# Unread products between TensorE's last mixing product, two global maxima and the down projection, and a sixth quantised tile ahead of the first gate/up evacuation

## The chip, the cores and the metric

One core of one Trainium2 chip runs the whole kernel. The metric is device microseconds of one execution, from the first to the last instruction and what lies around them. The kernel before took 748.6 us (median of three runs, 746.82 to 748.89 us).

## The reference

The kernel computes one layer of a graph network on 1250 nodes of width 1024, in float32. The parts ahead of the change (layer norm, a graph convolution over 40000 edges, linear attention with 16 heads) end in the matrix `x2`, the sum of both branches and the input. The change lies behind that, in the quantised feed-forward part:

```python
    def _L0_ffn_ref(x, clip_x, clip_down, w_gate, w_up, w_down):
        def _act_fake_quant(x, clip_factor):
            scale = jax.nn.sigmoid(clip_factor) * jnp.max(jnp.abs(x)) / QMAX
            return jnp.clip(_ste_round(x / scale), -QMAX - 1.0, QMAX) * scale
        ...
        xq = _act_fake_quant(x, clip_x[0])
        gate = jnp.einsum('bsh,ih->bsi', xq, _weight_fake_quant(w_gate))
        up = jnp.einsum('bsh,ih->bsi', xq, _weight_fake_quant(w_up))
        h = _act_fake_quant(jax.nn.silu(gate) * up, clip_down[0])
        return jnp.einsum('bsi,hi->bsh', h, _weight_fake_quant(w_down))
```

The width inside is 352. Both activations are quantised with one scale for the whole matrix: the maximum over all 1250 rows has to be known before the first element can be rounded. These are the two global maxima.

## The kernel before

The nodes lie in ten tiles of 128 rows (`T`; the last has 98). Every engine has its own program (`@block.sync`, `gpsimd`, `tensor`, `scalar`, `vector`), runs it in order, and waits on semaphores. The order of the work is written out by hand.

**Mixing.** `tile_b` (L690 on TensorE, L1280 on VectorE) runs for each tile 40 aggregation products (L698) and 48 attention products (L724). VectorE moves the second result out at L1317, and forms the tile's row extremes (L1328). GpSimd computes one column at L482, VectorE ends with the largest deviation.

**First maximum.** After the last tile VectorE writes the per-row maxima onto a diagonal (L1336, semaphore `m_ready`). TensorE multiplies it with a matrix of ones (L738), which puts all 1250 row maxima in every partition of bank 2. VectorE reduces them (`broadcast_max`, L1350: L1353, L1354) and computes each tile's scale and shift (L1358, `xn_columns`).

**Quantising.** `xq_tile(t)` on VectorE (L1361) scales a tile to int8 (L1366) and casts it to bf16 (L1371, `q_ready`). For the tiles in `ON_ACT` (1, 5, 7, 9) ScalarE does the scaling (`affine`, L932, L936). Tiles 0 and 1 are transposed by TensorE (`xq_tile`, L741, L745) and moved by ScalarE (L941). Tiles 2 to 9 are transposed by DMA, issued by SyncE as soon as `q_ready` allows (L391).

**Gate and up.** There are twelve units, numbered by `UNIT` (L254): four groups of columns `NCH` (256 columns are tiles 0 and 1; 512 are tiles 2 to 5; 256 are 6 and 7; 226 are 8 and 9) by three blocks of the inner width. `gate_up(u)` on TensorE (L748) runs 8 products for gate and 8 for up (L763). The first unit of a group waits for all of the group's tiles, and unit u waits until unit u-2 has been moved out. ScalarE applies silu to the gate (L953), VectorE multiplies it with up (`up`, L1383, L1391) and takes the maximum (L1380). Two lists set the order of quantising and units: `PE_FFN` for TensorE and ScalarE, `DVE_FFN` for VectorE (L261, L262).

**Second maximum and down.** VectorE reduces the maxima of the units (L1399, L1400, `m_ready`), TensorE broadcasts them (L773), VectorE reduces (L1353) and quantises the first 128 columns (L1402, L1406, `hq_first`). ScalarE quantises the others (L964, L966). TensorE then runs six products for each tile (L785) into `y_bank`, eight banks in turn: 0, 1, 6, 7, 2, 3, 4, 5. VectorE moves each half out (L1415), and VectorE (L1418) and GpSimd (L491) add 304 and 720 of the 1024 columns to `x2`, which SyncE stores.

Bank 3 holds half of the down weights' scales until ScalarE has moved them out at L929 (semaphore `d_row`, awaited by TensorE at L729, in the last tile's mixing). After that nothing is in it until the third tile of the down projection.

Of the kernel before, what the change touches and what calls it, by code (L numbers as in the profile page):

```python
# [17 lines left out]
HALF = 512  # L18
N, D = 1250, 1024
T = -(-N // P)  # L20
# [33 lines left out]
def gps_layer(nc, x, src, dst, gnn_W, gnn_b, Wq, bq, Wk, bk, Wv, bv, Wo, bo,  # L54
              clip_x, clip_down, w_gate, w_up, w_down, out):
    with ExitStack() as ctx:
        def sb(name, shape, dt):
            return ctx.enter_context(nc.sbuf_tensor(name, shape, dt))

        def sems(*names):  # L60
            return {n: ctx.enter_context(nc.semaphore(n)) for n in names}

        bank = [ctx.enter_context(nc.psum_tensor(f"bank{i}", [P, HALF], F32)) for i in range(8)]
# [8 lines left out]
        def part(at, *dims, dt=F32):  # L72
            size = 1
            for d in dims:
                size *= d
            words = size * {F16: 2, BF16: 2, I8: 1}.get(dt, 4) // 4
            a = mem[:, at:at + words]
            if dt != F32:
                a = a.bitcast(dt)
            if len(dims) == 2:  # L80
                a = a.rearrange("p (a b) -> p a b", b=dims[1])
            if len(dims) == 3:
                a = a.rearrange("p (a b c) -> p a b c", b=dims[1], c=dims[2])
            return a
# [38 lines left out]
        wdT = part(at, FB, D, dt=BF16)  # L123
# [41 lines left out]
        ident16 = sb("ident16", [P, P], BF16)  # L165
# [4 lines left out]
        def col(n=1):  # L170
# [16 lines left out]
        S = sems("consts", "pool_step", "edges_in", "bias_in", "x_in0", "x_in1", "dve_step",  # L187
                 *[f"w_in{i}_{c}" for i in range(8) for c in range(2)], "ln_step", "var_ready", "rstd_ready", "edges_ready",
                 "edges_T", "columns", "scratch_set", "ln_done", "xT_full", "xT_hi", "xT_lo", "w_hi", "w_lo", "kv_full", "kv_evac",
                 "k_relu", "kv_done", "q_full", "x_hi", "x_lo", "xT_in0", "xT_in1", "src_gap", "hot_src_act", "counts_diag", "q_relu", "q_hi", "q_lo", "g_full", "h_hi", "h_lo", "hot_dst_ready",  # L190
                 "hot_src_ready", "adj_mm", "adj_added", "counts_set")
# [5 lines left out]
        SF = sems("raw_in0", "raw_in1", "wq_ready", "w16_ready", "wT_in0", "wT_in1", "diag", "drow_full")  # L197
# [3 lines left out]
        def over_tiles(tile):  # L201

            for t in range(T):
                tile(t, t % 2, t // 2)
# [45 lines left out]
        landed = [16 * sum(1 if kind == "gu" else 2 for kind, _, _ in pieces[i % 2:i + 1:2]) for i in range(len(pieces))]  # L250
# [3 lines left out]
        UNIT = [(c, b) for c in range(len(NCH)) for b in range(FB)]  # L254
# [4 lines left out]
        Q = [("q", t) for t in range(T)]  # L259
        U = [("u", u) for u in range(len(UNIT))]  # L260
        PE_FFN = Q[:2] + U  # L261
        DVE_FFN = Q[:5] + U[:1] + Q[5:6] + U[1:3] + Q[6:8] + U[3:4] + Q[8:] + U[4:]  # L262

        AFFINE_AFTER = {("q", 1): 5, ("u", 1): 7, ("u", 2): 9}
        ON_ACT = (1, 5, 7, 9)
# [230 lines left out]
        def _(pe):  # L496
# [131 lines left out]
            with pe.If(span >= W):  # L628
                with pe.Fori(1, WINDOWS) as k:
                    with pe.Fori(0, C) as c:  # L630
                        pe.wait_ge(SE["e_hot"], 2 * ((k - 1) * C + c) + 2)
                        pe.matmul(agg[0][:, 0:WC], hot_src[0:EC, 0, 0, :], hot_dst[0:EC, 0, 0, :], start=True,
                                  stop=True).then_inc(SE["e_mm"], 1)
# [28 lines left out]
            for n in range(2):  # L662
                for p in range(PAIRS):
                    i = PAIRS * n + p
# [7 lines left out]
                    for a, b in ((0, 0), (0, 1), (1, 0)):  # L672
                        last = pe.matmul(m_bank[i % 4][:, :], kvs[:, a * PAIRS + p, :], wo16[n][p // 4][:, 2 * (p % 4) + b, :],  # L673
                                         start=(a == b), stop=(a == 1))
# [15 lines left out]
            def tile_b(t, par, t2):  # L690
# [25 lines left out]
                for n in range(2):  # L716
# [11 lines left out]
                    if (t, n) == (T - 1, 0):  # L728
# [5 lines left out]
            most = pe.value_load(flags[0:1, 1:2], min_val=0, max_val=E + 1)  # L734
            over_tiles(tile_b)

            pe.wait_ge(SC["m_ready"], 1)
            pe.matmul(bank[2][:, P:P + LAST], ones_m[0:LAST, :], max_diag[0:LAST, 1, 0:LAST], start=True,  # L738
                      stop=True).then_inc(SC["m_all"], 1)

            def xq_tile(t):  # L741
                o = tp[t % 2][:, :].bitcast(BF16)
                pe.wait_ge(SC["q_ready"], t + 1)
                for k in range(K):
                    last = pe.transpose(o[:, k * P:(k + 1) * P], q16[t % 4][:, k * P:(k + 1) * P], ident16[:, :])  # L745
                last.then_inc(SC["qT_full"], 1)

            def gate_up(u):  # L748
                c, b = UNIT[u]
                (c0, w), n = NCH[c], FR[b]  # L750
                pair = (bank[0:2], bank[6:8])[u % 2]
                if b == 0:
                    for t in range(c0 // P, -(-(c0 + w) // P)):
                        if t < 2:
                            pe.wait_ge(SC["qT_moved"], t + 1)
                        else:
                            pe.wait_ge(SC[f"qT_in{t % 4}"], 16 * ((t + 2) // 4))
                if u >= 2:
                    pe.wait_ge(SC["silu"], u - 1)
                    pe.wait_ge(SC["up_moved"], u - 1)  # L760
                for m in range(2):
                    for k in range(K):
                        last = pe.matmul(pair[m][0:n, 0:w], wguT[:, 2 * k + m, b * P:b * P + n],  # L763
                                         xqT[:, k, c0:c0 + w], start=(k == 0), stop=(k == K - 1))
                    last.then_inc(SC["gate_full"], 1)

            pe.wait_ge(S["counts_diag"], T + 1)
            for i in (8, 9):
                pe.wait_ge(SF[f"wT_in{i % 2}"], landed[i])
            for what, i in PE_FFN:  # L770
                xq_tile(i) if what == "q" else gate_up(i)
            pe.wait_ge(SC["m_ready"], 2)
            pe.matmul(bank[2][:, 0:P], ones_m, max_diag[:, 0, :], start=True, stop=True).then_inc(SC["m_all"], 1)  # L773

            for t in range(T):
                if t == 0:
# [194 lines left out]
        def _(dve):  # L971
# [389 lines left out]
            def xq_tile(t):  # L1361

                if t in ON_ACT:
                    dve.wait_ge(SC["affine"], ON_ACT.index(t) + 1)
                else:
                    step(dve.tensor_scalar(q8[t % 4], x2[:, t, :], xn_scale[:, t:t + 1], xn_shift[:, t:t + 1], ALU.mult, ALU.add))  # L1366
                if t in (4, 5):
                    dve.wait_ge(SC["qT_full"], t - 3)
                elif t >= 6:
                    dve.wait_ge(SC[f"qT_in{t % 4}"], 16 * ((t - 2) // 4))  # L1370
                dve.tensor_copy(q16[t % 4], q8[t % 4]).then_inc(SC["q_ready"], 1)  # L1371
# [11 lines left out]
            def up(u):  # L1383

                c, b = UNIT[u]
                (c0, w), n = NCH[c], FR[b]
                if u == 0:
                    dve.wait_ge(SC["gus"], 1)
                dve.wait_ge(SC["gate_full"], 2 * u + 2)
                dve.wait_ge(SC["silu"], u + 1)  # L1390
                dve.scalar_tensor_tensor(hT[0:n, b, c0:c0 + w], (bank[1], bank[7])[u % 2][0:n, 0:w],  # L1391
                                         gus[0:n, FB + b:FB + b + 1], sg[0:n, u % 2, 0:w], ALU.mult,
                                         ALU.mult).then_inc(SC["up_moved"], 1)
                h_max(u)

            for what, i in DVE_FFN[1:]:
                xq_tile(i) if what == "q" else up(i)
# [43 lines left out]
```

## Time and profile before

| | us |
|---|---|
| median of three runs | 748.6 |
| lowest and highest | 746.82, 748.89 |
| the profiled execution's own time | 748.37 |
| its span, first to last instruction | 746.6 |
| last mixing product ends | 675.98 |
| first product of gate and up starts | 687.26 |
| last product of gate and up ends | 716.32 |
| first product of down starts | 720.08 |

The lower part of the table is in microseconds from the span's start, as all times in the timelines are. The granted clock is the share of full speed (2.4 GHz) that TensorE was given: 1.00 and 0.50 (1.2 GHz) are its two levels here, and the mean over the span is 0.982. "Idle before" says how long an engine had nothing to run, and the arrow names whose work ended that.

### The profile page before, as it was taken

The numbers are of one execution on the slowest core, as the hardware profiler recorded it, in microseconds if no ns is written. First come the engines' busy times: TensorE is split into PE (matmuls) and PEld (weight loads), VectorE is DVE, ScalarE is ACT, GpSimd is POOL, SyncE is SP. The second block draws the span as 40 slices with busy tenths as digits, with TensorE's granted clock in tenths as the row PEclk, the third lists the DMA queues.
The fourth block names the chain that finished last, engine by engine and source line by source line (L and its number), as shares of the span: only waits on it lengthen the run. The fifth ranks groups of instructions, "written<-read, shape, count | busy, mean of one in ns | idle before, by whom it ended". The sixth has DMA issues, their size and how long they took to land.

```text
span 746.6 us, 12015 instructions
## 1 busy us (share of the span) xinstructions
PE 708.0 (95%) x3772; PEld 361.7 (48%) x3772; DVE 495.0 (66%) x975; ACT 209.5 (28%) x346; POOL 272.0 (36%) x403
## 2 busy tenths in 40 slices
PE   4999999999999999999999999999999999995984
PEld 2455555555555554666644444444444444443651
DVE  7878887887666655656842213657777788756667
ACT  5133334643333244446212212500000000012350
POOL 5566677898666655540010000011111111110018
PEclk9999999999999999999999999999999999996988
DMA  9652422541000000003030300242222222001406
GB/s 343 216 134 65 100 48 65 172 168 57 0 0 0 0 2 1 2 0 113 1 113 0 113 0 0 88 118 71 68 64 62 60 59 70 28 6 31 82 26 249
DMA packets 52764, 52.18 MB, mean 70 GB/s; under 512 B 36482, under 2 KB 37514, under 8 KB 52720
## 3 DMA queue, kind: packets, MB, share of 16 engines
q1 hardware_dynamic: 52720, 51.61, 22.9%
q8 instruction: 26, 0.43, 0.2%
q14 instruction: 18, 0.15, 0.1%
HBM read 37.96 MB, written 5.12 MB: 58 GB/s over the span
## 4 chain that ended last, share of the span: by engine, by line
PE 68%; issue 13%; DVE 9%; POOL 4%; ACT 2%; DMA 2%; DVEq 1%; POOLq 0%; SPq 0%; ACTq 0%
PE bank L532 31%; PE bank L724 12%; PE bank L698 10%; PE bank L606 10%; POOL mem L491 2%; DVE mem L1014 2%; PE bank L517 2%; ACT mem L812 2%; PE bank L549 2%; DVE counts L1104 1%; DVE mem L1184 1%; DMA mem<-in_x 1%; PE bank L673 1%; DVE mem L1030 1%; DMA mem<-in_L_gnn_W 1%
## 5 line engine op out<-in xcount | busy, mean ns | idle before, releaser
L532 PE MATMUL bank<-mem 128*128 128x512 f16 x1440 | 327.6, 381 | 4.9 <-DVE mem L1030 1.7
L532 PEld LDWEIGHTS bank<-mem 128*128 (+1 forms) x1440 | 137.9, 98 | 158.5 <-issue 6.9
L443 POOL TENSOR_SCALAR hot_src<-iota_p,src_col 125x128 bf16<-125x128 bf16 x252 | 174.3, 706 | 14.1 <-issue 14.1
L1104 DVE TENSOR_TENSOR counts<-bank,counts 128x120 f32 x328 | 92.4, 282 | 49.1 <-issue 8.4
L606 PE MATMUL bank<-mem 128*128 128x512 f16 (+2 forms) x576 | 105.3, 339 | 0.8 <-DVE mem L1143 0.8
L724 PE MATMUL bank<-mem 128*128 128x512 f16 x480 | 105.4, 379 | 0.0
L698 PE MATMUL bank<-mem 128*128 128x512 f16 x400 | 88.0, 379 | 0.0
L606 PEld LDWEIGHTS bank<-mem 128*128 128x128 f16 (+1 forms) x576 | 55.2, 98 | 42.5 <-DVE mem L1143 1.4
L724 PEld LDWEIGHTS bank<-mem 128*128 128x128 f16 x480 | 47.0, 98 | 55.7
L832 ACT ACTIVATE src_gap<-iota_p,loT 125x128 bf16<-125x128 bf16 x84 | 33.7, 402 | 114.4 <-PE bank L517 105.8
L480 POOL TENSOR_TENSOR mem<-mem 128x1024 f32<-128x1024 f32 x10 | 23.5, 2348 | 114.4 <-DMA mem<-in_L_mix_bo 114.4
L482 POOL TENSOR_TENSOR cols<-cols 128x1 f32<-128x1 f32 x10 | 5.6, 555 | 159.7 <-DVE cols L1326 159.7
L698 PEld LDWEIGHTS bank<-mem 128*128 128x128 f16 x400 | 39.2, 98 | 47.0
L1235 DVE SCALAR_TENSOR_TENSOR mem<-bank,cols,mem 128x512 f16<-128x512 f32 x20 | 14.9, 750 | 67.6 <-ACT mem L896 67.6
L1091 DVE TENSOR_TENSOR hot_dst<-iota_w,keyT 125x480 bf16<-125x480 bf16 x84 | 55.1, 657 | 0.0
L440 POOL COPY src_col<-loT 125x3 f32 (+1 forms) x84 | 25.7, 305 | 69.7 <-PE bank L517 64.9
L1014 DVE SCALAR_TENSOR_TENSOR mem<-mem 128x2048 f16<-128x2048 f32 x16 | 36.8, 2304 | 6.8 <-ACT mem L812 6.8
L896 ACT ACTIVATE mem<-bank,cols 128x512 f16<-128x512 f32 x20 | 13.8, 689 | 86.1 <-PE bank L532 76.6
L1317 DVE SCALAR_TENSOR_TENSOR mem<-bank,mem 128x512 f32<-128x512 f32 x20 | 13.8, 692 | 36.3 <-PE bank L724 36.0
L491 POOL TENSOR_TENSOR mem<-mem 128x720 f32<-128x720 f32 (+1 forms) x10 | 18.7, 1897 | 45.7 <-DVE mem L1415 45.7
L812 ACT ACTIVATE mem<-mem 128x2048 f16<-128x2048 f32 x16 | 30.4, 1906 | 15.4 <-DMA mem<-in_L_mix_Wk 6.1
L835 ACT ACTIVATE hot_src<-src_gap,cols 125x128 bf16<-125x128 bf16 x84 | 33.9, 404 | 2.7
(148 smaller groups left out, 644.4 us busy)
## 6 DMA issues: line engine op xcount, KB each, us to landing
mem<-in_x SPq DMA_DIRECT2D x18, 512.0 KB, 3.8
out_x<-mem SPq DMA_DIRECT2D x9, 512.0 KB
mem<-in_L_mix_Wk SPq DMA_DIRECT2D x4, 1024.0 KB, 9.5
mem<-in_L_mix_Wv SPq DMA_DIRECT2D x4, 1024.0 KB, 8.6
mem<-in_L_mix_Wq SPq DMA_DIRECT2D x4, 1024.0 KB, 5.2
mem<-in_L_gnn_W SPq DMA_DIRECT2D x4, 1024.0 KB, 5.2
mem<-in_L_mix_Wo SPq DMA_DIRECT2D x2, 2048.0 KB, 7.9
mem<-in_L_ffn_w_down SPq DMA_DIRECT2D x4, 352.0 KB, 3.1
```

The costliest lines, as they stand in the source:

```text
L443: pool.tensor_scalar(hot_src[0:EC, i, c, :], iota_p[0:EC, :], src_col[0:EC, i, c:c + 1], None, ALU.is_equal).then_inc(S["hot_src_ready"], 1)
L491: pool.tensor_tensor(x2[:, t, s], x2[:, t, s], y_t[t % 4][:, s], ALU.add).then_inc(SC["y_ready1"], 1)
L532: last = pe.matmul(o[:, :], xT[:, a * K + k, bass.ds(t * P, P)], w16[i][:, k, b, :], start=(at == 0), stop=(at == len(parts) - 1))
L606: last = pe.matmul(proj[j % 2][:, 0:w], w_q.rearrange("p a n -> p (a n)"), xT[:, a * K + k, t0 * P:t0 * P + w], start=(k == 0 and a == b), ...
L698: last = pe.matmul(agg[n][:, :], a_t[par][:, s, :], h16[:, s, b * D + n * HALF:b * D + (n + 1) * HALF], start=(fresh and s == 0 and b == 0 ...
L724: last = pe.matmul(proj[n][:, :], q_k, m16[b][:, k, n * HALF:(n + 1) * HALF], start=(k == 0 and a == b), stop=(k == K - 1 and a == 1))
L812: act.activation(w16[i][:, 4 * c:4 * c + 4, 0, :], w_raw[i][:, 4 * c:4 * c + 4, :], ACT.Copy, scale=W_UP).then_inc(S["w_hi"], 1)
L832: act.activation(src_gap[0:EC, i, :], iota_p[0:EC, :], ACT.Abs, bias=loT[0:EC, bass.ds(g * G + G - 1, 1)], scale=-1.0).then_inc(S["src_gap ...
L835: act.activation(hot_src[0:EC, i, G - 1, :], src_gap[0:EC, i, :], ACT.Relu, bias=ones[0:EC], scale=-1.0).then_inc(S["hot_src_act"], 1)
L1014: dve.scalar_tensor_tensor(w16[i][:, s, 1, :], w_raw[i][:, s, :], W_UP, w16[i][:, s, 0, :], ALU.mult, ALU.subtract).then_inc(S["w_lo"], 1)
L1091: dve.tensor_tensor(hot_dst[0:EC, i], iota_w[0:EC], key, ALU.is_equal).then_inc(S["hot_dst_ready"], 1)
L1104: dve.tensor_tensor(window, agg[i][:, k * WC:(k + 1) * WC], window, ALU.add).then_inc(S["adj_added"], 1)
```

## The change

It defines `keep_busy(n)`: n products of 128 x 512 (`ident16` as weights, the first 512 columns of the down weights `wdT` as the moving operand) that are written to bank 3 and that nobody reads. TensorE runs 19 of them between the last mixing product and L738, 11 between L738 and the transposes of tiles 0 and 1, 5 between these and the first unit, 6 before L773 and 6 after it. TensorE's waits for the constants and the last weight transposes (L767 to L769) come ahead of the first 19, since these read both. In `DVE_FFN` the sixth quantised tile comes ahead of unit 0 rather than behind it.

```diff
-        DVE_FFN = Q[:5] + U[:1] + Q[5:6] + U[1:3] + Q[6:8] + U[3:4] + Q[8:] + U[4:]
+        DVE_FFN = Q[:6] + U[:3] + Q[6:8] + U[3:4] + Q[8:] + U[4:]
...
+            def keep_busy(n):
+
+                for _ in range(n):
+                    pe.matmul(bank[3][:, :], ident16[:, :], wdT[:, 0, 0:HALF], start=True, stop=True)
+
+            pe.wait_ge(S["counts_diag"], T + 1)
+            for i in (8, 9):
+                pe.wait_ge(SF[f"wT_in{i % 2}"], landed[i])
+            keep_busy(19)
             pe.wait_ge(SC["m_ready"], 1)
...
-            pe.wait_ge(S["counts_diag"], T + 1)
-            for i in (8, 9):
-                pe.wait_ge(SF[f"wT_in{i % 2}"], landed[i])
-            for what, i in PE_FFN:
-                xq_tile(i) if what == "q" else gate_up(i)
+            keep_busy(11)
+            for i in range(2):
+                xq_tile(i)
+            keep_busy(5)
+            for u in range(len(UNIT)):
+                gate_up(u)
+            keep_busy(6)
             pe.wait_ge(SC["m_ready"], 2)
             pe.matmul(bank[2][:, 0:P], ones_m, max_diag[:, 0, :], start=True, stop=True).then_inc(SC["m_all"], 1)
+            keep_busy(6)
```

The order of TensorE's instructions from the last mixing product to the down projection; the kernel before, where L724 is mixing, L738 and L773 are the two maxima, L745 the transposes, L763 gate and up, L785 down:

```order
L724 MATMUL bank<-mem 128x512 x24
L738 MATMUL bank<-mem 128x98
L745 MATMUL bank<-ident,mem 128x128 x16
L763 MATMUL bank<-mem 128x256 x32
...
L763 MATMUL bank<-mem 96x226 x16
L773 MATMUL bank<-mem 128x128
L785 MATMUL bank<-mem 128x512 x60
```

The same place in the changed kernel (its line numbers are 9 to 12 higher; L740 are the unread products):

```order
L724 MATMUL bank<-mem 128x512 x24
L740 MATMUL bank<-mem,ident 128x512 x19
L747 MATMUL bank<-mem 128x98
L740 MATMUL bank<-mem,ident 128x512 x11
L754 MATMUL bank<-ident,mem 128x128 x16
L740 MATMUL bank<-mem,ident 128x512 x5
L772 MATMUL bank<-mem 128x256 x32
...
L772 MATMUL bank<-mem 96x226 x16
L740 MATMUL bank<-mem,ident 128x512 x6
L784 MATMUL bank<-mem 128x128
L740 MATMUL bank<-mem,ident 128x512 x6
L797 MATMUL bank<-mem 128x512 x60
```

Five groups, 47 products in all, stand between the others; nothing else on TensorE moved.

VectorE in the kernel before, from the cast of tile 3 on (L1366 and L1371 quantise, L1391 and L1380 evacuate a unit):

```order
L1371 CAST mem<-mem 128x1024
L1366 TENSOR_SCALAR mem<-mem,cols 128x1024
L1371 CAST mem<-mem 128x1024
L1391 SCALAR_TENSOR_TENSOR mem<-bank,cols,mem 128x256
L1380 TENSOR_REDUCE cols<-mem 128x1
L1371 CAST mem<-mem 128x1024
L1391 SCALAR_TENSOR_TENSOR mem<-bank,cols,mem 128x256
```

The same in the changed kernel (the lines are 12 higher):

```order
L1383 CAST mem<-mem 128x1024
L1378 TENSOR_SCALAR mem<-mem,cols 128x1024
L1383 CAST mem<-mem 128x1024 x2
L1403 SCALAR_TENSOR_TENSOR mem<-bank,cols,mem 128x256
L1392 TENSOR_REDUCE cols<-mem 128x1
L1403 SCALAR_TENSOR_TENSOR mem<-bank,cols,mem 128x256
```

The cast of tile 5 stands directly behind that of tile 4 instead of behind unit 0. SyncE's order is the same in both kernels.

## Rows read from the trace of the kernel before

**Rows 1.** The page: busy time of each engine.
```profile
PE 708.0 (95%) x3772; PEld 361.7 (48%) x3772; DVE 495.0 (66%) x975; ACT 209.5 (28%) x346; POOL 272.0 (36%) x403
```
**Rows 2.** Stretches of 0.5 us: length, engines' busy time, PEclk, DMA share, GB/s.
```profile
678.00:678.50 0.50, 0.00 (x0) 0.00 (x0) 0.50 (x2) 0.00 (x0) 0.41 (x1) 0.76 0.00 0
...
691.50:692.00 0.50, 0.50 (x4) 0.37 (x3) 0.50 (x2) 0.00 (x0) 0.00 (x0) 0.58 0.24 48
...
719.00:719.50 0.50, 0.00 (x0) 0.00 (x0) 0.50 (x3) 0.01 (x1) 0.00 (x0) 0.72 0.00 0
...
726.00:726.50 0.50, 0.50 (x4) 0.23 (x3) 0.50 (x3) 0.50 (x1) 0.25 (x1) 0.95 0.00 0
```
**Rows 3.** Timeline around the first maximum: start, length, engine, line, operation, idle before.
```profile
673.66 2.32 PE L724 MATMUL bank<-mem 128*128 128x512 f16 x10
...
680.50 0.75 PE L738 MATMUL bank<-mem 98*128 98x98 f32 x2 [4.52 <-DVE mem L1336]
681.36 0.39 DVE L1353 TENSOR_REDUCE cols<-bank 128x1 f32<-128x226 f32 x1 [0.84 <-PE bank L738]
...
683.28 0.69 DVE L1371 CAST mem<-mem 128x1024 bf16<-128x1024 int8 x1
...
684.12 1.87 PE L745 MATMUL bank<-ident,mem 128*128 128x128 bf16 x16 [2.87 <-DVE mem L1371]
```
**Rows 4.** Timeline from the transposes to the first unit of 512 columns.
```profile
685.17 1.94 ACT L941 ACTIVATE mem<-bank 128x1024 bf16<-128x1024 bf16 x2 [1.55 <-PE bank L745]
...
687.00 1.24 ACT L936 ACTIVATE mem<-mem,cols 128x1024 int8<-128x1024 f32 x1
...
687.26 7.66 PE L763 MATMUL bank<-mem 128*128 128x256 bf16 x48 [1.27 <-ACT mem L941]
...
688.43 0.69 DVE L1371 CAST mem<-mem 128x1024 bf16<-128x1024 int8 x1
...
690.93 0.48 DVE L1391 SCALAR_TENSOR_TENSOR mem<-bank,cols,mem 128x256 f32<-128x256 f32 x1 [1.81 <-PE bank L763]
...
691.79 0.68 DVE L1371 CAST mem<-mem 128x1024 bf16<-128x1024 int8 x1
...
695.91 4.26 PE L763 MATMUL bank<-mem 128*128 128x512 bf16 x19 [1.00 <-DMA mem<-mem]
```
**Rows 5.** The DMA transposes of the quantised tiles (L391), one line's view.
```profile
L391 SPq DMA_TRANSPOSE mem<-mem x8: 1231/1232/1521, 686.3 to 703.8; - x8
...
DMA to landing us min/median/max: 3.1/3.2/3.3
```
**Rows 6.** Timeline: 48 products of 512 columns in a row at full clock.
```profile
645.80 10.52 PE L724 MATMUL bank<-mem 128*128 128x512 f16 x48
```
**Rows 7.** Timeline from the last units to the second maximum and the down projection.
```profile
699.80 16.52 PE L763 MATMUL bank<-mem 128*128 128x512 bf16 x126
...
717.80 0.49 PE L773 MATMUL bank<-mem 128*128 128x128 f32 x2 [1.48 <-DVE mem L1400]
718.32 0.29 DVE L1353 TENSOR_REDUCE cols<-bank 128x1 f32<-128x128 f32 x1 [0.58 <-PE bank L773]
...
720.08 16.12 PE L785 MATMUL bank<-mem 128*128 128x512 bf16 x60 [1.79 <-DVE mem L1406]
...
721.52 0.84 ACT L966 ACTIVATE mem<-mem 128x768 bf16<-128x768 int8 x1
721.58 0.75 DVE L1415 SCALAR_TENSOR_TENSOR mem<-bank,cols,mem 128x512 f32<-128x512 f32 x1 [1.56 <-PE bank L785]
...
723.69 1.87 POOL L491 TENSOR_TENSOR mem<-mem 128x720 f32<-128x720 f32 x1 [45.04 <-DVE mem L1415]
...
726.25 16.79 POOL L491 TENSOR_TENSOR mem<-mem 128x720 f32<-128x720 f32 x9 [0.69 <-DVE mem L1415]
726.47 1.40 DVE L1415 SCALAR_TENSOR_TENSOR mem<-bank,cols,mem 128x512 f32<-128x512 f32 x2
```

## The prediction

> **What bounds the kernel now.** The page comes first: TensorE is busy for 708.0 of 746.6 us [rows 1], so nearly everywhere it sets the pace, and only its gaps and its clock are open to a change like this. Next the granted clock in stretches of 0.5 us [rows 2]. In the part that the change touches it falls twice. The first fall is in the stretch 678.0 to 678.5 us, with TensorE idle since 675.98 [rows 3]; the clock is back only at 691.9. The second fall is between 719.0 and 719.5, after an idle time that only L773 interrupted for 0.49 us [rows 7]; it is back at 726.0. In both cases TensorE then runs real work at 1.2 GHz: L738, the transposes and the first units of gate and up, and later two tiles of the down projection. Last the timelines, to see which of this ends a wait.
>
> Around the first maximum everything is one chain: product L738, VectorE's reduction and scaling, the first cast, the transposes, ScalarE's move, and gate/up at 687.26 [rows 3, 4]. TensorE then runs three units of 256 columns, and waits 1.00 us for a DMA before the first unit of 512 columns at 695.91 [rows 4]. That DMA is the transpose of tile 5. Behind it TensorE has no gap until 716.32 [rows 4, 7]. So all that matters of the first half is how far the start at 695.91 moves. In the down projection GpSimd's addition starts at 723.69, idles once for 0.69 us until 726.25, and then runs nine tiles without a gap [rows 7]; VectorE keeps the same pace of 1.9 us for a tile. There the end is set by when the first two tiles are delivered.
>
> **The unread products themselves.** At full clock a product of 512 columns takes 10.52 / 48 = 0.22 us [rows 6]. Nineteen are 4.2 us: from 675.98 to 680.2, and L738 could not start before 680.50 anyway. This is hidden, with 0.3 us to spare. L738 then ends near 680.9; eleven are 2.4 us, to 683.3, and the first cast delivers tile 0 not before 683.6 (below). Five are 1.1 us behind the second transposes (685.0 to 686.1), while ScalarE is still moving. Six are 1.3 us in the 1.48 us gap before L773, and six again in the 1.79 us gap behind it [rows 7]. All 47 lie in gaps and cost nothing as long as the clock is full. Without that cover each costs its own 0.22 us, or 0.43 us at half clock, because TensorE runs in order. Their bank is free until the third tile of down, and the weights whose landing is now awaited earlier were transposed long before. I take the bank, the operands and the moved waits at nothing.
>
> **The first chain at full clock.** If the unread products keep the clock up:
> - L738 to the reduction took 0.86 us at half clock (680.50 to 681.36) [rows 3]. The same step at full clock is L773, 0.52 us (717.80 to 718.32) [rows 7]. Gain 0.34, which moves VectorE's whole quantising earlier by as much: the casts of tiles 0 to 4 stand back to back with their scalings. The cast of tile 0 ends at 683.97 - 0.34 = 683.63.
> - Eight transposes are 8 x 0.107 us at half clock and half that at full: 0.43 less ahead of ScalarE's first move. From the cast's end to ScalarE was 1.20 us (683.97 to 685.17) [rows 3, 4], and becomes 0.78, so ScalarE starts at 684.4. Its two moves take 1.94 us together, as before, and gate/up starts at 684.4 + 1.94 + 0.15 = 686.5 rather than 687.26.
> - A unit of 256 columns is 16 products: 3.5 us at half clock, 1.75 at full. Unit 0 ends at 688.25, unit 1 at 690.0. Unit 2 needs unit 0 moved out.
>
> **The moved tile.** VectorE's cast of tile 4 ended at 689.12 [rows 4], now 688.8. The next instruction is the cast of tile 5, 0.68 us, whose scaling ScalarE ends at 688.24 at the latest [rows 4], so it ends at 689.5. It used to stand behind unit 0 and ended at 692.47. Unit 0 is moved out from 689.5 to 690.0 instead of from 690.93: the cast ahead of it delays it, by up to 0.7 us against an evacuation in the old order at full clock. It holds back unit 2, which starts at 690.1 instead of 690.0, and units 1 and 2 end at 690.0 and 691.8. What is queued behind it on VectorE (units 1 and 2, tiles 6 and 7) is needed by TensorE only for unit 6, more than 10 us later. So the step costs nothing by itself.
>
> SyncE issues the transposes one behind the other, 1.23 us each, and each lands 3.2 us after its issue [rows 5]. Tile 4 is issued at 688.8, so tile 5 can follow at 690.05 and not at 689.5; it lands at 693.25. With 0.15 us for the wait, unit 3 starts at **693.4**, where it started at 695.91: gain **2.5 us**. Between bounds: if the transfers get in each other's way (they used to be 1.45 us apart, and 5 follows 4 after 1.25) it can be 0.5 us less; if SyncE's issue doesn't hold tile 5 back, 0.5 us more; and the very most is 4.1 us, when TensorE itself is ready at 691.8. I take 2.5, since both durations in it are rows of the same instruction.
>
> Behind unit 3 everything is TensorE's own time. Tiles 6 and 7 move out earlier with the rest, and the second maximum comes 2.5 us earlier.
>
> **The down projection at full clock.** VectorE started on the first half at 721.58, 1.50 us after the first product: three products at half clock (1.28) and 0.22 until seen. Now it is 3 x 0.22 + 0.2 = 0.86, i.e. 720.94 in the old times. The second half is complete 0.66 us later, VectorE has moved both by 722.35, and GpSimd starts at 722.42 instead of 723.69: 1.27 earlier. The second tile comes 1.9 us later, at 724.3, instead of at 726.25: **1.9 us** earlier, and the 0.69 us of idle time are gone. VectorE, whose third tile started at 726.47, starts it at 720.94 + 2 x 1.9 = 724.74, **1.7 us** earlier. The pace of 1.9 us for a tile remains, and becomes the bound from the first tile on. ScalarE's quantised columns for tiles 2 and 3 are ready at 722.36 [rows 7], and TensorE wants them at 720.08 + 12 x 0.22 = 722.72, so the next thing that is late has 0.36 us to spare. I take 1.8.
>
> **Sum.** 2.5 + 1.8 = 4.3 us. The profiled execution took 748.37 us, so 744.1; its own time lies 0.2 below the median of the runs (748.6), and I predict **744.2 us**, 0.6% less. A measurement of this kernel can tell about 0.3% (2.2 us) from no change; the three runs before lie 2.1 us apart.
>
> **Rivals.**
> 1. *The clock is lost in one of the two places.* The products leave gaps of 0.3 to 0.6 us, and around the transposes TensorE runs only about 0.45 us at a time: from 683.3 to 686.5 it is busy for about 2.0 of 3.2 us. L773 alone did not keep the clock at its fall of 719 [rows 2, 7]. For holding: after the third unit of 256 columns TensorE idled 1.00 us and the clock stayed [rows 2, 4]. If it is lost around the transposes, units 0 to 2 run largely at half clock as before, unit 3 waits for TensorE (686.9 + 7.8 = 694.7) and gains about 1.1; with down, 2.9, so 745.5. If it is lost around the second maximum, only the 2.5 remain: 745.9. The Trainium skill ("TensorE: Matmul & The Clock Gate", "A second HAM failure mode: psum-queue depth-cycling") describes a kernel whose short idles between groups of products made the clock swing between its levels; by that rule the outcome here would be this rival's 745.5 to 745.9. The trace does not bear it out: with 0.2 to 1 us idle at a time it shows no fall.
> 2. *Neither gap is held and only the order pays.* The products end before the awaited signals, and the clock falls in what is left. Then tile 5 is early but TensorE is not ready before 695.1 (687.26 + 7.66, and the wait): 0.8 to 1 us, so 747.5. Against it: the gaps left are a tenth of those at which it fell.
> 3. *Slower: the unread products run at half clock and stand in the way.* Were the clock to fall at 678.25 as before, ten products would be done and nine would take 0.43 each: L738 starts at 682.1, 1.6 late. Eleven take 4.7 us and five 2.15, so gate/up starts near 691.6; even at full clock from there unit 3 starts at 696.9, 1.0 late. Around the second maximum six take 2.6 us in 1.5 and in 1.8: 1.1 and 0.8 late. Together 2.9 slower, 751.3. It decides from the point where 19 products outlast 4.5 us, 0.24 us each. Against it: products of this very shape in the mixing keep the clock at 1.00, at 0.22 each, and these follow without a gap.
> 4. *More than forecast:* the transpose of tile 5 lands as soon as TensorE is ready, 691.9: 4.0 + 1.8, 742.5. Against it the issue time.
>
> **How the numbers follow.** Forecast 0.68; rival 1 0.14, rival 2 0.08, rival 3 0.05, rival 4 0.05. The forecast's own range is 743.2 to 745.2 (0.5 us for the landing, 0.2 for down, the rest the scatter of a median). To hold 8 in 10 the range takes in most of rivals 1 and 4: 742.6 to 746.4. Faster by more than 0.3% is below 746.4: the forecast, rival 4 and two thirds of rival 1, 0.82. Within 0.3%: rival 2 and the rest of rival 1, 0.13. Slower: 0.05.
>
> **What would show it.** The granted clock stays at 1.00 from 676 us to the end of the down products. Fifteen or more of the first nineteen products take 0.22 us each, and L738's successor starts within 0.1 us of the signal. Gate/up starts 0.7 to 0.8 us earlier, unit 0's evacuation stands behind the cast of tile 5, and unit 3 starts at 693.4, still released by a DMA. GpSimd has no idle time between its first two additions. I am wrong if a stretch between 683 and 687, or the one before down, shows 0.50; if unit 3 is released by TensorE's own work; or if the last additions end less than 3.5 us earlier.

## The result, and the profile after

The changed kernel took 745.92 us (median of 15 runs, 744.61 to 747.70), the kernel before 748.40 us in the 15 runs beside them. The ratio is 0.9971, with a 95% interval of 0.9964 to 0.9979: 0.29% less, at the very edge of what the prediction called distinguishable. 744.2 us was predicted, in a range of 742.6 to 746.4. The time lies in the range, but not in the forecast's own 743.2 to 745.2; the gain is 2.5 us, and 4.2 to 4.3 were forecast. So the question is where 1.8 us went.

The page says that TensorE was busier, and clocked higher: the mean granted clock over the span is 0.992 instead of 0.982.

```profile
PE 713.9 (96%) x3819; PEld 363.7 (49%) x3819; DVE 494.7 (66%) x975; ACT 208.8 (28%) x346; POOL 270.9 (36%) x403
```

The timeline of the changed kernel around the first maximum (start, length, engine, line, operation, idle before). L740 are the unread products, L747 answers to L738, L754 to L745, L953 to L941 and L772 to L763 of [rows 3, 4]:

```profile
671.66 4.05 PE L724 MATMUL bank<-mem 128*128 128x512 f16 x18
...
675.54 4.26 PE L740 MATMUL bank<-mem,ident 128*128 128x512 bf16 x19
...
680.23 0.47 PE L747 MATMUL bank<-mem 98*128 98x98 f32 x2 [0.43 <-DVE mem L1348]
...
680.53 2.54 PE L740 MATMUL bank<-mem,ident 128*128 128x512 bf16 x11
680.80 0.39 DVE L1365 TENSOR_REDUCE cols<-bank 128x1 f32<-128x226 f32 x1 [0.56 <-PE bank L747]
...
683.48 0.62 PE L754 MATMUL bank<-ident,mem 128*128 128x128 bf16 x8 [0.41 <-DVE mem L1383]
...
684.13 1.94 ACT L953 ACTIVATE mem<-bank 128x1024 bf16<-128x1024 bf16 x2 [1.07 <-PE bank L754]
...
684.73 1.24 PE L740 MATMUL bank<-mem,ident 128*128 128x512 bf16 x5
...
686.21 5.41 PE L772 MATMUL bank<-mem 128*128 128x256 bf16 x48 [0.24 <-ACT mem L953]
```

The last mixing product ends at 675.71 here and at 675.98 before [rows 3], so 0.27 us are to be taken off every comparison of starts. With that, everything up to gate/up is as forecast: the unread products end in time, L747 hands over after 0.57 us instead of 0.86, ScalarE starts 0.77 us earlier (684.13 for 685.17), and gate/up starts 0.78 us earlier. Three units take 5.41 us instead of 7.66.

What follows is not. The same timeline on, from the evacuation of unit 0 to the start of unit 3, answering to [rows 4]:

```profile
687.87 1.29 DVE L1383 CAST mem<-mem 128x1024 bf16<-128x1024 int8 x2
...
689.08 0.48 DVE L1403 SCALAR_TENSOR_TENSOR mem<-bank,cols,mem 128x256 f32<-128x256 f32 x1
...
694.39 9.83 PE L772 MATMUL bank<-mem 128*128 128x512 bf16 x37 [2.77 <-DMA mem<-mem]
```

TensorE is through with unit 2 at 691.62 and then waits 2.77 us for the transpose of tile 5; before, it waited 1.00. The view of the transposes' line, of which the first four are those that unit 3 needs, says that one of them took 4.8 us, and SyncE's issue of one 2.3 us; [rows 5] had 3.3 and 1.5 as the largest:

```profile
L391 SPq DMA_TRANSPOSE mem<-mem x8: 1232/1320/2297, 685.7 to 704.0; - x8
...
DMA to landing us min/median/max: 3.2/3.2/4.8
```

The granted clock (columns as in [rows 2]) is 1.00 from 676 to 695.5 us, through both gaps that the change fills. Then it falls, in a place where it had not fallen before:

```profile
695.50:696.00 0.50, 0.50 (x3) 0.17 (x2) 0.00 (x0) 0.00 (x0) 0.00 (x0) 0.72 1.11 213
...
699.00:699.50 0.50, 0.50 (x3) 0.24 (x2) 0.00 (x0) 0.00 (x0) 0.00 (x0) 0.86 0.00 0
```

TensorE had idled 2.77 us and had then worked for 1.3. From 695.7 to 699.1 unit 3 runs at 1.2 GHz, eight products at twice 0.22 us.

Around the second maximum and in down the clock is 1.00 and the timeline is as forecast. The answer to [rows 7]:

```profile
718.29 1.46 PE L740 MATMUL bank<-mem,ident 128*128 128x512 bf16 x6
...
720.25 13.21 PE L797 MATMUL bank<-mem 128*128 128x512 bf16 x60 [0.50 <-DVE mem L1418]
...
721.11 1.41 DVE L1427 SCALAR_TENSOR_TENSOR mem<-bank,cols,mem 128x512 f32<-128x512 f32 x2 [0.92 <-PE bank L797]
...
722.59 18.70 POOL L491 TENSOR_TENSOR mem<-mem 128x720 f32<-128x720 f32 x10 [44.23 <-DVE mem L1427]
```

GpSimd's ten additions now have no gap. From the first product of down to the end of the last addition it was 22.96 us (720.08 to 743.04) and is 21.04: 1.92 less.

The account of the two profiled executions (spans 746.6 and 744.8 us): 0.27 ahead of the change, 1.25 earlier at unit 3 (695.91 against 694.39, less the 0.27), 1.68 lost again up to the end of the units (20.41 us from unit 3 to 716.32 before, 22.09 to 716.48 now), 1.92 gained in down. Together 1.76, and the spans differ by 1.8. In this pair of executions the first half of the change was thus worth minus 0.4 us, and all of the gain is the second half's. The changed kernel's profiled execution took 746.61 us, 0.7 more than its median, so others lost less.

### The profile page after: what moved, and what is told of

Its sections match the earlier page's. It is cut to its first block, busy times and chain, and to the rows that moved or that the text cites. A ratio compares the mean times of both kernels' runs of the same rounds, so it can differ in the third digit from the quotient of the medians.

```text
span 744.8 us, 12108 instructions
## 1 busy us (share of the span) xinstructions
PE 713.9 (96%) x3819; PEld 363.7 (49%) x3819; DVE 494.7 (66%) x975; ACT 208.8 (28%) x346; POOL 270.9 (36%) x403
## 4 chain that ended last, share of the span: by engine, by line
PE 69%; issue 12%; DVE 9%; POOL 4%; ACT 2%; DMA 2%; DVEq 1%; POOLq 0%; SPq 0%; ACTq 0%
PE bank L532 31%; PE bank L724 13%; PE bank L698 10%; PE bank L606 10%; POOL mem L491 2%; DVE mem L1026 2%; PE bank L517 2%; ACT mem L824 2%; PE bank L549 2%; DVE counts L1116 1%; DVE mem L1196 1%; PE bank L673 1%; DMA mem<-in_x 1%; DVE mem L1042 1%; DMA mem<-in_L_gnn_W 1%
## 5 line engine op out<-in xcount | busy, mean ns | idle before, releaser
L724 PE MATMUL bank<-mem 128*128 128x512 f16 x480 | 105.4, 379 | 0.0
L724 PEld LDWEIGHTS bank<-mem 128*128 128x128 f16 x480 | 46.9, 98 | 55.8
L517 PEld LDWEIGHTS bank<-hot_dst,hot_src 125*128 125x128 bf16 x328 | 24.5, 97 | 20.7 <-POOL hot_src L443 1.3
```

The lines of the kernel that those rows point to most:

```text
L517: last = pe.matmul(agg[i][:, c * WC:(c + 1) * WC], hot_src[0:EC, i, c, :], hot_dst[0:EC, i, c, :], start=(c == 0), stop=True, skip_group_c ...
L724: last = pe.matmul(proj[n][:, :], q_k, m16[b][:, k, n * HALF:(n + 1) * HALF], start=(k == 0 and a == b), stop=(k == K - 1 and a == 1))
```

## The experiments

Two things were to be explained: the clock fall behind unit 3, and the transfer that was 1.3 us late (694.39, where 693.4 was forecast, which is 693.1 in this execution's times). The ratios are to the kernel before, timed beside them on the same chip.

**Nine more unread products in the wait for tile 5.**

```diff
             for u in range(len(UNIT)):
+                if u == FB:
+                    keep_busy(9)
                 gate_up(u)
```

> The changed kernel with nine more unread products (2.0 us at full clock) between unit 2 and unit 3, where TensorE waited 2.77 us for the transpose of tile 5 and its clock fell 1.2 us after the wait's end. Theory A (that wait lets the clock fall, and unit 3 at half clock costs the gain): no fall behind unit 3, unit 3's first eight products take 1.8 us instead of 3.4, and the time is 1.5 to 1.8 us under that of the changed kernel, 744.3 us. Theory B (the fall does not depend on that wait): the same time as the changed kernel, 745.9, or later by what the nine products outlast the DMA.

745.18 us (744.88 to 746.50), ratio 0.9966 (0.9952 to 0.9979). In the profiled execution the clock is 1.00 from 676 to 732 us, and the unit starts as late as before but does not slow down. The timeline and two stretches of it:

```profile
691.69 2.10 PE L740 MATMUL bank<-mem,ident 128*128 128x512 bf16 x9
694.26 9.01 PE L772 MATMUL bank<-mem 128*128 128x512 bf16 x41 [0.46 <-DMA mem<-mem]
```
```profile
694.00:696.00 2.00, 1.74 (x9) 0.82 (x10) 0.88 (x2) 0.00 (x0) 0.00 (x0) 1.00 0.26 52
696.00:698.00 2.00, 2.00 (x11) 0.94 (x10) 0.09 (x1) 0.69 (x1) 0.00 (x0) 1.00 1.03 194
```

Its span is 743.0 us, 1.8 under the changed kernel's profiled 744.8: theory A, to the size. The median moved only 0.7 us, less than the two intervals can tell apart, and two of the five runs are at 746.0 and 746.5 with a mean clock of 0.991; where the clock fell in those is not known. So the mechanism is shown in the trace, and the timing does not decide.

**The old order of VectorE's work, with all unread products.**

```diff
-        DVE_FFN = Q[:6] + U[:3] + Q[6:8] + U[3:4] + Q[8:] + U[4:]
+        DVE_FFN = Q[:5] + U[:1] + Q[5:6] + U[1:3] + Q[6:8] + U[3:4] + Q[8:] + U[4:]
```

> The changed kernel with the old DVE_FFN: all unread products, but the cast of tile 5 again behind unit 0. Theory A (the DMA of tile 5 ends TensorE's wait, so its cast counts): the cast ends 0.9 us later (689.16 plus an evacuation of 0.48 and a maximum of 0.42), its transfer lands 0.3 to 0.9 us later, and so does the time: 746.2 to 746.8 us. Theory B (the transfers queue up behind one another, so the place of the cast is worth nothing): 745.9 us.

746.52 us (745.20 to 747.26), ratio 0.9974 (0.9964 to 0.9984). That is the size that theory A gives, but the intervals of the two kernels overlap, so the timing doesn't settle it. In the profile unit 3 starts at 694.73 after 2.72 us of waiting, 8.12 us behind the start of gate/up; in the changed kernel it is 8.18. In this execution the place of the cast bought nothing. The tile's transfer was late in both for another reason, below.

**Only the first gap filled, and only the second.** The first kernel is the changed one without the six and six products around the second maximum; the second is the kernel before with only these (TensorE's moved waits stay in their new place).

```diff
-            keep_busy(6)
             pe.wait_ge(SC["m_ready"], 2)
             pe.matmul(bank[2][:, 0:P], ones_m, max_diag[:, 0, :], start=True, stop=True).then_inc(SC["m_all"], 1)
-            keep_busy(6)
```

> The changed kernel without the six and six unread products around the second maximum. Theory A (the two halves of the gain are independent, and the second is the down projection at full clock): the clock falls near 719, GpSimd's second addition waits 0.7 us again, and 1.7 to 1.9 us are lost: 747.7 us. Theory B (the clock would have held without them, since its fall near unit 3 has shifted when it is judged): 745.9 us.

747.49 us (746.58 to 750.04), ratio 0.9992 (0.9983 to 1.0001): no gain that can be measured. The loss against the changed kernel is 1.6 us, near theory A's 1.7 to 1.9. In the profiled execution the clock fell around unit 3, as in the changed kernel, this time 0.2 us before the end of a wait of 2.58 us (unit 3 starts at 695.53):

```profile
694.00:696.00 2.00, 0.47 (x2) 0.22 (x3) 1.94 (x3) 0.00 (x0) 0.00 (x0) 0.83 0.31 58
```

Yet around the second maximum, where theory A wants it, it did not fall. The view of the stretches from the end of the units on:

```profile
717.00:719.00 2.00, 0.52 (x7) 0.28 (x4) 1.29 (x4) 0.21 (x1) 0.00 (x0) 1.00 0.00 0
719.00:721.00 2.00, 0.47 (x2) 0.28 (x2) 1.35 (x6) 0.32 (x1) 0.00 (x0) 1.00 0.00 0
721.00:723.00 2.00, 1.73 (x8) 0.79 (x9) 1.08 (x3) 1.94 (x4) 0.00 (x0) 1.00 0.00 0
```

The gaps are those at which it fell before the change (1.48 and 1.80 us, a product of 0.49 between them), and this time it stayed. One and the same gap can thus end either way; what decides it was not found. In this execution down took 21.05 us from its first product to the end of the last addition, as in the changed kernel, and the span less the 1.3 us by which mixing ended later is not longer than the changed kernel's: with the clock up, leaving the products out costs nothing. That the 1.6 us of the median come from executions in which the clock fell here is thus likely, and not shown. The ten other runs have mean clocks of 0.988 to 0.991.

> The kernel before with only the six and six unread products around the second maximum. Theory A: down at full clock alone, 1.8 to 1.9 us under the kernel before, 746.6 us, and within 0.8 us of the whole change, whose first half gave nearly nothing. Theory B (the clock is given back before down anyway, or VectorE's pace hides it): less than 0.8 us.

746.88 us (746.25 to 747.37), ratio 0.9984 (0.9975 to 0.9993), 1.4 under the kernel before. Theory A's sign and place, three quarters of its size. It is 1.0 us from the whole change, where 0.8 was expected. The two halves together (0.8 and 1.6 per mille) make 2.4 of the whole's 2.9. In the profiled execution down took 21.05 us again. A likely reason why the medians give less than 1.8 is seen in two other kernels without products here, the order alone and the regrouped one without unread products (both below): their clock also fell at the second maximum, but was back 3.4 us later, at 722.99 and 722.88, and not after 6.8 us as in [rows 2]. The order alone:

```profile
719.60 14.86 PE L785 MATMUL bank<-mem 128*128 128x512 bf16 x60 [1.80 <-DVE mem L1406]
723.21 18.71 POOL L491 TENSOR_TENSOR mem<-mem 128x720 f32<-128x720 f32 x10 [44.66 <-DVE mem L1415]
```

That is 22.32 us for down, in both, instead of the 22.96 of the profiled kernel before: against the 21.05 at full clock the fall costs 1.3 us there in two traces, 1.9 in one, and nothing in the one where it doesn't come.

**More instructions in the same time.** The trace has one more thing to tell about the late transpose. In stretches of 0.5 us, in the changed kernel (the last two columns are the DMA engines' busy share and GB/s):

```profile
688.00:688.50 0.50, 0.50 (x7) 0.45 (x5) 0.50 (x2) 0.00 (x0) 0.00 (x0) 1.00 4.04 33
688.50:689.00 0.50, 0.50 (x7) 0.45 (x5) 0.50 (x2) 0.00 (x0) 0.00 (x0) 1.00 0.01 1
689.00:689.50 0.50, 0.50 (x7) 0.44 (x6) 0.50 (x2) 0.47 (x2) 0.00 (x0) 1.00 0.08 9
```

A share of 4 at 33 GB/s, where 0.77 goes with 137 GB/s in the next kernel's trace, means that packets stood far longer than they moved. After it the engines did next to nothing for a microsecond, with tile 3 on its way. The queue view of 687.5 to 690 us has a packet there that is no data of the kernel's:

```profile
q1 hardware_dynamic: 804, 0.20, 128.5%
q8 instruction: 1, 0.02, 3.2%
```

It is a fetch of some 16 KB of instructions (in the kernel before it runs alone: 66 GB/s over a quarter of a microsecond). There it fell between 692 and 694 us, in a pause of the transposes. The unread products of the first gap are 35 products with their weight loads, 70 instructions, and so the same fetch comes sooner. To move it again without moving anything else, the first 19 and 11 products were cut into 38 and 22 of half the width (`keep_busy` takes the width as its second argument).

```diff
-            keep_busy(19)
+            keep_busy(38, HALF // 2)
...
-            keep_busy(11)
+            keep_busy(22, HALF // 2)
```

> The changed kernel with 38 and 22 unread products of 256 columns in place of 19 and 11 of 512: the same time on TensorE, but 60 instructions more (each product has its weight load) ahead of gate/up, so that the 16 KB fetch of instructions that fell at 688 us, in the middle of the transpose of tile 3, comes before the first transpose starts. Theory C (that fetch and the transpose stop one another: the transpose landed after 4.8 us instead of 3.2, and the later ones with it): no transpose takes over 3.4 us, unit 3 starts about 1.0 us earlier, at 693.4, TensorE's wait shrinks from 2.8 to 1.8 us; the time is 1.0 us lower, or 2.7 if the clock then survives the shorter wait, 744.9 to 743.2 us. Theory D (the four transposes delay each other whenever they follow at 1.3 us): a landing of 4.5 us or more stays, and 745.9 us.

745.03 us (744.08 to 745.35), ratio 0.9966 (0.9954 to 0.9978). The fetch now lies between 680 and 682 us, the same stretch of 688 us has no hole, and the first four transposes land in 3.2 to 3.5 us. Their view, and TensorE's timeline:

```profile
688.00:688.50 0.50, 0.50 (x7) 0.44 (x6) 0.47 (x2) 0.00 (x0) 0.00 (x0) 1.00 0.77 137
688.50:689.00 0.50, 0.50 (x7) 0.45 (x5) 0.50 (x2) 0.00 (x0) 0.00 (x0) 1.00 0.94 190
```
```profile
L391 SPq DMA_TRANSPOSE mem<-mem x4: 1231/1232/1338, 685.9 to 690.1; - x4
...
DMA to landing us min/median/max: 3.2/3.3/3.5
```
```profile
686.40 5.41 PE L772 MATMUL bank<-mem 128*128 128x256 bf16 x48 [0.25 <-ACT mem L953]
693.59 12.60 PE L772 MATMUL bank<-mem 128*128 128x512 bf16 x67 [1.78 <-DMA mem<-mem]
```

The wait is 1.78 us, as theory C gave it, and the clock held; the span of 742.3 us is 2.5 under the changed kernel's. The median is 0.9 lower, but the ratio hardly differs from the changed kernel's 0.9971: the trace shows the mechanism, and the timing doesn't tell the two apart. One clause of theory C failed: "no transpose takes over 3.4 us" holds for those that unit 3 needs, give or take 0.1, but the next fetch fell at 702 us, beside the last transposes, and one of these took 4.6 us (nobody waited for it). That is the same coupling again. All thirteen traces side by side, with the first four transposes, TensorE's wait just before unit 3, and what the clock did around that wait:

| kernel | fetch, us | longest of the first four | idle before unit 3 | clock |
|---|---|---|---|---|
| before | 692.5, between tiles 4 and 5 | 3.3 us | 1.00 us | held |
| only the second gap | 692.5, between tiles 4 and 5 | 3.3 us | 1.22 us | held |
| half width | 681 to 682 | 3.5 us | 1.78 us | held |
| half width and seven more, below | 681 to 682 | 3.5 us | 0.25 us | held |
| changed kernel | 687.5 | 4.8 us | 2.77 us | fell, 1.3 us after the wait |
| changed kernel, again | 688.0 | 4.6 us | 2.49 us | fell, 0.8 us after the wait |
| old order | 688.0 | 4.7 us | 2.72 us | fell, 1.0 us after the wait |
| only the first gap | 688.5 | 4.7 us | 2.58 us | fell, 0.2 us before its end |
| nine more products | 687.5 | 4.5 us | 0.46 us | held |
| only the order, below | 693.0, on tile 5 | 4.8 us | 0.39 us | held |
| regrouped, below | 688.0 | 4.7 us | none | held |
| regrouped, half width, below | 681 to 682 | 3.3 us | none | held |
| regrouped, no unread, below | 693.0, on tile 5 | 4.7 us | none | held |

In the eight traces with the fetch among these transposes one of them is late, in the five others none is. The clock fell in the four with an idle time of 2.49 us or more and in none with 1.78 or less; in all four it was back 3.4 us later, and the units from unit 3 on took 21.97 to 22.09 us instead of the 20.40 that the same grouping takes without a fall.

**Only the order.**

```diff
-        DVE_FFN = Q[:5] + U[:1] + Q[5:6] + U[1:3] + Q[6:8] + U[3:4] + Q[8:] + U[4:]
+        DVE_FFN = Q[:6] + U[:3] + Q[6:8] + U[3:4] + Q[8:] + U[4:]
```

> The kernel before with only the new DVE_FFN, no unread products. By the prediction's second rival TensorE at half clock is not ready before 695.1, so unit 3 gains 0.8 us: 747.6 us. A rival: the cast in front of unit 0 costs what it gives, 748.4 us.

747.18 us (746.52 to 747.90), ratio 0.9994 (0.9985 to 1.0003): 0.6 us where 0.8 was expected, but not told apart from nothing. The transpose of tile 5 was issued 2.2 us earlier than before and then met the fetch, so that unit 3 started at 695.43, after 0.39 us of waiting; TensorE alone would have been ready at 695.04.

**Both causes treated.** Half-width products, and seven products of 512 columns in the 1.8 us that are left before unit 3, with the changed kernel again on the same chip.

> The changed kernel once more, beside the next two on one chip. If its spread (744.61 to 747.7 us in 15 runs) comes from where its clock falls, the runs lie between 744.6 and 747.7 again, those with a granted clock of 0.995 or more at the lower end, around a median of 745.9 us; and the profile shows the wait for tile 5 again, at 2.4 to 2.9 us.

> The kernel with 38 and 22 unread products of 256 columns, and seven of 512 (1.5 us) in the 1.8 us before unit 3. Both causes of the lost gain are then treated: the fetch lies ahead of the transposes, and TensorE has no idle time above 0.5 us from the last mixing product to the end. This is the kernel that the prediction described: 744.1 us, with a spread under 1 us. If the unread products themselves cost something that the sum left out, it stays above 744.7 us.

The changed kernel: 746.01 us (744.31 to 747.56, 11 runs), ratio 0.9968 (0.9958 to 0.9978), with a wait of 2.49 us in the profile. The treated kernel: 744.63 us (744.24 to 744.85), ratio 0.9955 (0.9941 to 0.9968). It is 1.4 us lower, though the intervals of the ratios still overlap, and the runs spread over 0.6 us (5 runs) instead of 3.3 (11 runs). TensorE's timeline in it:

```profile
686.55 5.41 PE L772 MATMUL bank<-mem 128*128 128x256 bf16 x48 [0.25 <-ACT mem L955]
691.80 1.67 PE L740 MATMUL bank<-mem,ident 128*128 128x512 bf16 x7
693.73 12.48 PE L772 MATMUL bank<-mem 128*128 128x512 bf16 x66 [0.25 <-issue]
```

Its span is 742.5 us; the prediction's sum is 746.6 - 4.3 = 742.3. In the changed kernel the two runs with a mean clock of 0.996 took 744.3 and 744.8 us, as in the first 15, where the two such runs took 744.75 and 744.84: those may be the runs in which the fall behind unit 3 didn't happen; none of them has a trace, so this is not shown. Runs at 0.992 lie between 744.6 and 747.6, so the mean clock alone does not sort them.

**Groups that need fewer tiles.** Instead of filling the wait it can be taken away: units 3 to 5 get 256 columns (tiles 2 and 3), units 6 to 8 get 512 (tiles 4 to 7).

```diff
-NCH = [(0, 256), (256, 512), (768, 256), (1024, N - 1024)]
+NCH = [(0, 256), (256, 256), (512, 512), (1024, N - 1024)]
...
-        DVE_FFN = Q[:6] + U[:3] + Q[6:8] + U[3:4] + Q[8:] + U[4:]
+        DVE_FFN = Q[:6] + U[:2] + Q[6:8] + U[2:6] + Q[8:] + U[6:]
```

> The changed kernel with the second group of columns cut to 256 and the third widened to 512 (tiles 2 and 3, then 4 to 7), and the quantising of tiles 6 and 7 behind unit 1. Unit 3 then needs only tiles 2 and 3. If what is lost is all in the wait for tile 5 and the clock fall behind it, TensorE goes from unit 2 to 3 without a wait, waits under 0.5 us before unit 6, no clock falls, and 2.8 + 1.7 less up to 0.5 us are gained: 741.9 us. If the wait only moves to unit 6 (tile 7 lands at 696.9 or later): 743.5 to 745.9 us.

742.89 us (742.58 to 743.81), ratio 0.9939 (0.9925 to 0.9952): twice the gain of the change, 1.0 us short of the expectation. TensorE has no wait for a transfer any more (136 products recorded in one stretch, with 4.7 us for one transpose that nobody feels), and the clock stays at 1.00:

```profile
686.67 19.71 PE L772 MATMUL bank<-mem 128*128 128x256 bf16 x136 [0.24 <-ACT mem L953]
```
```profile
690.00:694.00 4.00, 3.92 (x36) 3.42 (x35) 3.86 (x9) 3.17 (x4) 0.00 (x0) 1.00 1.02 197
694.00:698.00 4.00, 3.98 (x34) 3.35 (x34) 2.33 (x6) 0.94 (x2) 0.00 (x0) 1.00 0.69 131
```

> Both edits: groups of 256, 256, 512 and 226 columns, and the 60 instructions more. If the fetch matters only through the wait for a transpose, it adds nothing to the regrouped kernel where that has no wait left: 741.9 us, within 0.5 us of it. If the regrouped kernel still waits for tile 7, this takes up to 1.0 us off.

743.19 us (742.69 to 743.49), ratio 0.9943 (0.9929 to 0.9956). All transposes land within 3.3 us, and the time is the same within 0.3 us: without a wait for them the fetch costs nothing.

> The kernel before with the groups of 256, 256, 512 and 226 columns and the new place of tiles 6 and 7, and no unread products. At half clock TensorE is ready for unit 3 at 695.1 and does not wait; the 0.8 us of the order alone, or a little more since unit 3 to 5 need no transfer: 747.2 to 747.6 us. If so, the regrouping pays only beside the unread products, since these make the transfers the bound. If the regrouping is a gain by itself, under 746.5 us.

747.10 us (746.52 to 747.57), ratio 0.9987 (0.9978 to 0.9996), within 0.1 us of the order alone. At half clock TensorE is the later one, and the grouping adds nothing that can be measured. The regrouping is worth 3 us only beside the unread products.

## Why the prediction was right and wrong

The time lies in the range by luck as much as by the sum. The range had been widened for a clock lost in one of the filled gaps, which did not happen; it was lost elsewhere, at a similar price. The prediction's own signs went against it: the clock did not stay at 1.00, and the last additions end 1.75 us earlier (741.29 for 743.04), where less than 3.5 was to count against it.

- **The unread products are free and hold the clock: right.** All 47 lie in the gaps, the clock is 1.00 from 676 to 695.5 us and from 699.5 to the last product of down. Rival 3 (half clock in the way) did not come, nor rival 2.
- **The first chain: right.** 0.29 for L738 (forecast 0.34), gate/up 0.78 earlier (0.76). The 0.107 us for a transpose stands in no row ([rows 3] give 1.87 us for 16, 0.117 each); from the cast's end to ScalarE it is 0.72 us now, 0.78 forecast.
- **The cast of tile 5: right in its own size** (two casts in a row, unit 0 moved out at 689.08, 689.2 forecast in this execution's times), and free.
- **The landing of tile 5: mis-sized.** The step "tile 5 can follow at 690.05 ... it lands at 693.25" took 3.2 us from eight transposes that had met no fetch of instructions. One of them took 4.8 us, SyncE's queue stood with it, and unit 3 started 1.3 us late. The prediction counted the unread products as time on TensorE alone; that their 70 instructions also move a fetch was left out. With the fetch moved away (half width) the wait was 1.78 us and unit 3 started at 693.59, 0.3 us after the forecast in that execution's times.
- **"Behind unit 3 everything is TensorE's own time": this is the sentence that failed.** It took for granted that the time is at full clock. The prediction itself had TensorE ready at 691.8 and unit 3 at 693.4, an idle time of 1.6 us, 0.6 more than the only gap that it could quote as harmless, and it never asked about the clock there. With the late transfer it became 2.77, and the clock fell. Price 1.68 us. It took both errors: the wait of 1.78 us in the half-width kernel, nearly the 1.6 of the prediction, did not lose the clock. The new wait stood exactly where the faster engine had been made to arrive early.
- **Down: right in the profile**, 1.92 for 1.8; alone it measured 1.4 in the medians. The 1.8 was read from one execution of the kernel before, in which the clock stayed low until 726.05. Two others show it back by 723, and there the whole fall costs 1.3. The term was the price of the dearest of the three falls, so that it came out in this pair of profiles is in part luck.
- **Rival 1** came nearest with its time (745.5 to 745.9), and with its idea, but it looked for the fall in the gaps that the change fills. Those were safe. The Trainium skill's rule that stood beside it ("TensorE: Matmul & The Clock Gate", "A second HAM failure mode: psum-queue depth-cycling", short idles between groups of products) is not what happened: with gaps of 0.2 to 0.5 us the clock held throughout the two filled gaps, and the fall went with one long wait for a DMA. Nor were the gaps left "a tenth of those at which it fell", as rival 2 has it: at the second maximum 0.19 and 0.50 us are left of 1.48 and 1.79. The same page's section "HAM oscillation — how this bites in real kernels" describes that other kind, products that wait for a DMA and lose the clock by it, and was the one to weigh.

The kernel with both causes treated gave 744.63 us for a forecast of 744.2, and its span of 742.5 us is within 0.2 of the sum. That bears out the sum for the two profiled executions. Between medians it is less: the kernel before took 747.93 us beside it, so the gain is 3.3 us and not 4.3, and of the missing 1.0 the cheaper falls in down can explain a part.

## What to carry to other kernels

When a stage is sped up, the engine arrives early at the next thing it depends on: compute that new wait, and ask of it everything that was asked of the old one, the clock included. Filling a wait with unread products keeps the clock but leaves the wait; shrinking what the next unit needs (two tiles instead of four) took both away and gave twice the gain. Where a gap's effect on the clock goes either way from run to run, the spread of the runs is a second sign: it was 3.3 us with the long wait (11 runs), and 0.6 and 1.2 us in two kernels without one (5 runs each). And a gain that is the price of such a fall is to be read from more than one execution of the kernel before.

## What the runs showed of the hardware

- A fetch of some 16 KB of instructions that falls among DMA transposes delays one of them by 1.2 to 1.5 us (among the first four 4.5 to 4.8 us to landing instead of 3.2 to 3.5, in eight traces of thirteen). In the changed kernel the engines then move almost nothing for about 1.2 us (10 GB/s at most). Moving the fetch by adding instructions in the same time removed the delay. Which of the two holds up the other was not tried. The Trainium skill ("Runtime: NRT & Kernel Launch", "Instruction fetch mechanics") describes fetches in blocks of 16 KiB, 256 instructions, which agrees with the packet of 0.02 MB in the trace; by that section the cost of a fetch is mostly hidden; here a transpose beside it was late, and unit 3 with it.
- At the first maximum the clock fell 2.3 us after the last product (before the change, from 675.98), but only 4.9 us after it, and after an idle time of 4.62 us, in the kernel with only the second gap filled. It fell 2.4 us into a wait of 2.58 us; around waits of 2.49, 2.72 and 2.77 us it fell 0.8 to 1.3 us after their end. It held over waits of 1.00, 1.22 and 1.78 us. Over 1.48 and 1.80 us with a short product between, it fell in three traces (before, only the order, regrouped without unread products) and held in one.
